# Order of slot and block products, first fetches, mix products and gate work in a graph and expert kernel

## What is computed

```
xn = layernorm(x)
h  = A @ xn                                # A: 3125 x 3125, sums edge weights (spmm)
z0 = softmax((A @ h)  @ W0.T + b0)         # 128 wide
z1 = softmax((A @ [z0, z0]) @ W1.T + b1)   # 128 wide
x  = x + tanh([z0, z1] + h) + mix(xn)      # mix: linear attention, q k v, per-head norms, wo
x  = x + ffn(layernorm(x))                 # 8 experts, gate picks one, capacity 489, 1024 hidden
```

## Time and profile before

| | us |
|---|---|
| median of 3 runs | 1150.28 |
| the profiled execution | 1142.74 |
| its span | 1141.0 |
| PE busy in the span | 1071.9 (94%) |
| PE's weight loads busy | 666.5 (58%) |
| DVE busy | 738.9 (65%) |
| ACT busy | 314.7 (28%) |
| POOL busy | 163.2 (14%) |
| first 25 iterations | about 15 to 216 |
| block products to their end | about 216 to 595 |
| layers 0 and 1 with the gate | about 600 to 902 |
| experts | about 913 to the end |

### The profile page before, as it was taken

How to read it: one execution, slowest core, us unless ns; L and a number is a source line. 1 busy time by engine, 2 the same in 40 slices (tenths; PEclk the granted TensorE clock), 3 DMA queues, 4 the chain that set the end, 5 groups by cost and what they waited for, 6 DMA issues and landing times.

```text
span 1141.0 us, 15390 instructions
## 1 busy us (share of the span) xinstructions
PE 1071.9 (94%) x5383; PEld 666.5 (58%) x5383; DVE 738.9 (65%) x1860; ACT 314.7 (28%) x1042; POOL 163.2 (14%) x208
## 2 busy tenths in 40 slices
PE   5869989999999999999979999999998799999995
PEld 3446656656666666666774444644458566666664
DVE  8978999998786887869950111217877445544444
ACT  4657867522222222222210111201112112222220
POOL 1113223301000000000000000000344511111111
PEclk9889999999999999999998999999999899999998
DMA  6111110111324333342348988987994665555510
GB/s 173 16 12 47 47 47 18 76 82 76 146 115 153 122 133 136 131 167 105 139 160 314 361 309 301 358 319 281 311 327 171 179 194 125 136 137 133 147 51 8
DMA packets 78877, 178.60 MB, mean 157 GB/s; under 512 B 33567, under 2 KB 62011, under 8 KB 66639
## 3 DMA queue, kind: packets, MB, share of 16 engines
q1 hardware_dynamic: 67550, 126.16, 34.4%
q10 hardware_dynamic: 7120, 43.34, 9.4%
q0 software_dynamic: 4128, 8.08, 2.0%
HBM read 116.23 MB, written 63.77 MB: 158 GB/s over the span
## 4 chain that ended last, share of the span: by engine, by line
PE 77%; DVE 11%; SPq 4%; issue 4%; ACT 2%; DMA 1%; POOLq 0%; POOL 0%; ACTq 0%; DVEq 0%
PE ps L1720 21%; PE ps L1571 20%; PE ps L1820 10%; PE ps L1808 9%; PE ps L1555 7%; SPq L477 2%; PE ps L1595 2%; PE ps L1530 2%; PE ps L1463 1%; PE ps L1516 1%; PE ps L1550 1%; DVE RING L1096 1%; DVE RING L1087 1%; DVE W L1039 1%; SPq L475 1%
## 5 line engine op out<-in xcount | busy, mean ns | idle before, releaser
L1571 PE MATMUL ps<-RING,XX 128*128 128x512 f32 (+2 forms) x700 | 297.1, 550 | 2.0 <-DVE W L1103 2.0
L1720 PE MATMUL ps<-RING,RY 128*128 128x512 f32 (+4 forms) x750 | 272.1, 520 | 5.7 <-issue 5.7
L1720 PEld LDWEIGHTS ps<-RING,RY 128*128 128x128 f32 x750 | 135.7, 194 | 125.7 <-issue 118.3
L790 ACT COPY RING<-ps 128x512 f32<-128x512 f32 (+3 forms) x163 | 91.0, 559 | 291.6 <-PE ps L1555 266.3
L1571 PEld LDWEIGHTS ps<-RING,XX 128*128 128x128 f32 x700 | 118.1, 191 | 69.9 <-issue 62.1
L1096 DVE TENSOR_TENSOR RING<-RING,RY 128x768 bf16<-128x768 bf16 x275 | 142.7, 560 | 4.0
L1555 PEld LDWEIGHTS ps<-RING 128*128 128x128 bf16 x1575 | 100.6, 97 | 50.0 <-issue 43.3
L1087 DVE TENSOR_TENSOR RING<-iota_p,RY 128x512 bf16<-128x512 bf16 x275 | 114.1, 456 | 18.1 <-PE ps L1555 15.7
L1555 PE MATMUL ps<-RING 128*128 128x128 bf16 (+1 forms) x1575 | 112.9, 217 | 0.0
L916 ACT ACTIVATE RY<-ps,b1T 128x489 f32<-128x489 f32 x64 | 42.8, 669 | 172.4 <-PE ps L1808 172.4
L1436 DVE SCALAR_TENSOR_TENSOR W<-ps,RING,W 128x256 f32<-128x256 f32 (+1 forms) x32 | 15.5, 484 | 99.0 <-PE ps L1820 97.8
(11 more groups left out here) (265 smaller groups left out, 1313.5 us busy)
## 6 DMA issues: line engine op xcount, KB each, us to landing
RING<-adj_dram SPq DMA_DIRECT2D x60, 1280.0 KB, 6.4
adj_dram<-RING ACTq DMA_DIRECT2D x30, 1280.0 KB, 4.8
rbuf_dram<-W SPq DMA_DIRECT2D x8, 516.0 KB, 5.1
RING<-rbuf_dram SPq DMA_DIRECT2D x8, 516.0 KB, 4.0
xbuf_dram<-W SPq DMA_DIRECT2D x8, 512.0 KB, 3.2
XT<-in_L_ffn_w SPq DMA_DIRECT2D x16, 256.0 KB, 5.2
XT<-in_L_ffn_w SPq DMA_DIRECT2D x4, 1024.0 KB, 8.6
RING<-in_L_ffn_w SPq DMA_DIRECT2D x16, 256.0 KB, 4.5
```

Of the source, the lines that this page charges most:

```text
L790: nc.scalar.copy(RING[:, n % 2, at:at + w], ps[:, u % 2, 0:w]).then_inc(s_bev, 1)
L1571: last = nc.tensor.matmul(ps[:, ACC + dd, 0:w], XN[:, j, dd * H:(dd + 1) * H], at[:, i * w:(i + 1) * w], start=(j == 0), stop=True, skip_g ...
L1720: last = nc.tensor.matmul(o, (Y if l == 0 else S0)[:, j, :], RING[:, slot_of[g % 5], i * across + first:i * across + first + w], start=(j ...
```

## The change

Six edits of order; no operation's size changes.
1. PE does slots(it-1) behind build(it-3), and kvprod ahead of turn. ACT's kept goes behind evac.
2. On SP's queue, five weight loads (wo, wq, W0, W1, b1) leave the place behind window group 1 and are issued by ACT in iteration 1; eleven small loads move from behind group 1 to behind group 2.
3. Mixes 16 to 24 (HELD = 16) come after the last block product, each in its own half bank; before, mixes 0 to 21 stood in the loop and 22 to 24 behind it. DVE's additions of these wait until a bank holds all its mixes, and come last. turns of layer 0, strips 0 and 1, wait for all additions.
4. ACT does zout(1, kc) ahead of exp8(ka) and xtout(kb).
5. In layer 1, counts(ka-1) and gate_turn(ka) leave strip kb for strip kc; turns(1, kb) and logits(ka) go from tiles 4 and 5 of strip kc to tile 13.
6. counts(ka) and gate_turn(kb) leave strip kc and follow turns(1, kc).

```diff
-MIX_AT = {40 + 4 * _m: _m for _m in range(NT - 3)}
+HELD = 16
+MIX_AT = {40 + 4 * _m: _m for _m in range(HELD)}
...
-        mix_bank = lambda m: MIXB if m < NT - 2 else ACC + m - (NT - 2)
+        HELD_AT = ((MIXB, 0), (MIXB, D), (KVACC, 0), (KVACC, D), (PROD, 0), (PROD, D), (ACC, 0), (ACC, D), (ACC + 1, 0))
+
+        def mix_out(m):
+            bank, at = HELD_AT[max(m - HELD, 0)]
+            return ps[:, bank, at:at + D]
+
+        def mixes_to_bank(m):
+            return m + 1 if m < HELD else max(n for n in range(HELD, NT) if HELD_AT[n - HELD][0] == HELD_AT[m - HELD][0]) + 1
...
-                if g == 1:
-                    for to, src in ((wo_n, half("L0_mix_wo")), (wq_n, half("L0_mix_wq")), (W0_n, a["L0_gnn_W0"]),
-                                    (W1_n, a["L0_gnn_W1"]), (b1_n, a["L0_ffn_b1"])):
-                        sp.dma_start(to, src).then_inc(s_wt5, 16)
+                if g == 2:
...
                 if it < NT:
                     turned(it)
+                if it == 1:
+                    for to, src in ((wo_n, half("L0_mix_wo")), (wq_n, half("L0_mix_wq")), (W0_n, a["L0_gnn_W0"]),
+                                    (W1_n, a["L0_gnn_W1"]), (b1_n, a["L0_ffn_b1"])):
+                        act.dma_start(to, src).then_inc(s_wt5, 16)
...
-                if 1 <= it <= NT:
-                    kept(it - 1)
                 if 0 <= u < NU:
                     evac(u)
...
+                if 1 <= it <= NT:
+                    kept(it - 1)
...
+            zout(1, kc)
             exp8(ka)
             xtout(kb)
-            zout(1, kc)
...
             def mixed(m):
-                dve.wait_ge(s_mixp, m + 1)
+                dve.wait_ge(s_mixp, mixes_to_bank(m))
                 dve.wait_ge(s_bo, m + 1)
-                v.tensor_tensor(X1[:, m, :], X1[:, m, :], ps[:, mix_bank(m), 0:D], ALU.add).then_inc(s_mrd, 1)
+                v.tensor_tensor(X1[:, m, :], X1[:, m, :], mix_out(m), ALU.add).then_inc(s_mrd, 1)
...
-            mixed(NT - 3)
             hn_out(NT - 2)
-            mixed(NT - 2)
             hn_out(NT - 1)
-            mixed(NT - 1)
+            for m in range(HELD, NT):
+                mixed(m)
...
-                if 1 <= it <= NT:
-                    slots(it - 1)
...
                     build(it - BUILD_IT)
+                if 1 <= it <= NT:
+                    slots(it - 1)
+                if KV_LAG <= it < NT + KV_LAG:
+                    kvprod(it - KV_LAG)
                 if it + 1 < NT:
                     turn(it + 1)
-                if KV_LAG <= it < NT + KV_LAG:
-                    kvprod(it - KV_LAG)
...
-            mix(NT - 3)
+            mix(HELD)
             hidden_node(NT - 2)
-            mix(NT - 2)
+            mix(HELD + 1)
             hidden_node(NT - 1)
-            mix(NT - 1)
+            for m in range(HELD + 2, NT):
+                mix(m)
...
+                if l == 0 and k < 2:
+                    pe.wait_ge(s_mrd, NT)
...
-            strip(1, kb, {3: [later(turns, 1, ka)], 4: [later(logits, ka - 1)], 14: [later(counts, ka - 1)], 22: [later(gate_turn, ka)]})
-            strip(1, kc, {4: [later(turns, 1, kb)], 5: [later(logits, ka)], 21: [later(counts, ka), later(gate_turn, kb)]})
+            strip(1, kb, {3: [later(turns, 1, ka)], 4: [later(logits, ka - 1)]})
+            strip(1, kc, {4: [later(counts, ka - 1)], 6: [later(gate_turn, ka)], 13: [later(turns, 1, kb), later(logits, ka)]})
             turns(1, kc)
+            counts(ka)
+            gate_turn(kb)
             logits(kb)
```

More of the change, by code:

```diff
@@ L1591, in mix @@
                 pe.wait_ge(s_mv, 1)
-                if m < NT - 2:
-                    ge(pe, s_mrd, m)
+                ge(pe, s_mrd, min(m, HELD))
                 for c in range(2):
-                    last = nc.tensor.matmul(ps[:, mix_bank(m), 0:D], XT[:, c, m * P:(m + 1) * P], M[:, c, :], start=(c == 0), stop=(c == 1))
+                    last = nc.tensor.matmul(mix_out(m), XT[:, c, m * P:(m + 1) * P], M[:, c, :], start=(c == 0), stop=(c == 1))
                 last.then_inc(s_mixp, 1)
```

## The result

The changed kernel takes 1136.47 us (median of 4 runs, 1133.77 to 1137.01) against 1150.36: ratio 0.9875, 95% interval 0.9855 to 0.9896, 13.9 us less. The prediction said 1137.3, 13.0 less.

A forecast was written before the change was run, and what follows sets the result against it. PE was taken as the bound, nearly full in the first 25 iterations and the long middle; 7.6 - 0.9 + 2.8 + 3.5 = 13.0 us off the 1150.28 median gave 1137.3, range 1133 to 1145.5.

The forecast's parts named there:

- (a): First fetches at the start: window group 2 is issued earlier and DVE's wait goes; 7.6 us, between 4 and 8.5.
- (b): Order in the first 25 iterations: build fills slots' waits, turn waits for kept; -0.9 us, between -4 and +2.5.
- (d): Gate work at the end of layer 1: the last biased(kc) starts 3.8 us earlier; taken as 3.5, between 1.5 and 4.5.
- 5.96: DVE's idle before head_scale at the start, expected to go with the earlier window group 2, bringing slots(5) 5.96 us earlier.
- 2.2 - 0.17: By product(7): build(3) no longer follows slots(5), 2.2 us won, less 0.17 for turn's new wait.
- the collision: ACT's five weight loads run beside window group 1's last windows; a delay of 0 to 1.7 us possible, 0.4 taken.
- rival 2: Starts collide, holding group 1's windows by 1.7, and small terms fall short: gain about 7 us, 1143.3; chance 0.21.
- a turn wait of 0.17: From product(7) to product(24), turn waits 0.17 for ACT's kept in each of 17 iterations: 2.9 us lost.
- The 0.33 at each chunk end: At four chunk ends ACT's store, issued ahead of kept, delays turn by 0.33 each: 1.3 us lost.
- (c): Mixes held back behind the block products: 1.3 us from a longer lead, 1.5 from the branch; 2.8, between 0 and 5.3.
- the drain of the chunk traffic: Behind the block products: chunk loads and stores end earlier relative to the branch on `rounds`, shortening it by 1.5 us.
- Rival 1: PE's sequencer could hold 32 pairs, so nearly all the 5.66 us gap goes: 2.5 us more, 1134.8; chance 0.10.

The follow-up runs named there:

- again: Changed kernel without any edit, run again on the second chip: 1127.58 us against 1142.90 for the kernel before, ratio 0.9859.
- five_sp: Changed kernel with the five weight loads back on SP's queue behind window group 1, second chip: 1126.51 us, ratio 0.9850.
- woven: The kernel both, with turn behind the first of apply's four matmuls from iteration 4 on: 1129.44 us, ratio 0.9818.
- held_only: Kernel before with only mixes 16 to 24 moved behind the last block product: 1145.96 us, ratio 0.9954.
- gate_only: Kernel before with only the moved gate work of layer 1's last strips: 1146.85 us, ratio 0.9965.
- after: First profiled execution of the changed kernel, span 1132.0 us; that kernel's median is 1136.47 us, ratio 0.9875.
- fetch_only: Kernel before with only the new order of first fetches (five weight loads, eleven small loads): 1148.12 us, ratio 0.9979.
- order_only: Kernel before with only the new order of the first 25 iterations (slots, kvprod, kept): 1147.74 us, ratio 0.9975.
- again2: Changed kernel without any edit, run a third time, on the third chip: 1136.31 us against 1151.26, ratio 0.9870.
- both: Changed kernel with the five weight loads back on SP and ACT's chunk store behind kept, third chip: 1133.02 us, ratio 0.9845.
- held20: Changed kernel with HELD = 20, so 12 pairs behind the last wait in place of 28: gap 4.94 us, no total time given.
- late_store: Changed kernel with ACT's chunk store issued behind kept and not ahead of it: 1125.07 us, ratio 0.9842.
- held18: Changed kernel with HELD = 18, so 20 pairs behind the last wait in place of 28: gap 3.12 us, no total time given.

## Why the prediction was right

The sum was 13.0; like for like (before against `again`) the spans differ by 14.7, and the medians by 13.9 to 15.3. The step that saved it was to take the 13.0 off the median shown and not off the profiled execution: the 7.5 between the two is the pause in strips kb and kc, which the change neither makes nor takes away (last section). That the total came this close is in part luck: (a) fell short, and (b), (d) and the clock made up for it.

**(a) and (b), 6.7 forecast, 6.65 measured** at kvprod(20), and 2.4 + 2.9 = 5.3 by the single parts. The sum is right and the terms were not. By product(7), where (a) was to end, 81.53 - 75.10 = 6.4 had come of 7.6. Little of that is the fetch, for which I had 5.96. Product(7) is at 79.7 to 79.8 in three kernels with the old order, one of them with the new fetches, at 76.85 with the new order alone, and at 74.7 to 75.5 with both (five profiles). So about 1.8 of the 6.4 was the lateness of the one profile of before, 2.9 the order (I had 2.2 - 0.17) and 1.3 to 2.1 the fetches on top of it. The 5.96 was one execution's wait (1.83 to 5.42 in three others), and the collision was sized at 0.4 where ACT's cast came 1.4 to 2.2 late. That was the first condition of rival 2, and my own mark for a wrong prediction, cast(1) after 26.5, was passed (27.07, 27.48); `five_sp` prices it at 1.0. The error of (b) went the other way: behind product(7) 0.2 was won where I had -0.9. I charged a turn wait of 0.17 in 17 iterations, 2.9 us; the wait is there (0.20, and with `woven`'s order the products come 0.18 closer), but the new order also brought build and slots 0.16 closer together, so an iteration grew by 0.05. That 0.16 I had nowhere in the sum. The 0.33 at each chunk end was right in kind: the rows have 0.51 to 0.54, of which 0.20 is the ordinary wait.

**(c), 2.8 forecast, 2.9 measured** for the gap (5.66 to 2.76), 5.3 (3.3 to 7.2) by the ratio of `held_only` alone. The mechanism held, the split did not: the lead grew by 2.3 (forecast 1.3), and from the load of `rounds` to the first strip it takes 6.74 in place of 7.33, 0.6 less (forecast 1.5). The branch took 6.2 to 7.0 us in the four kernels with the old mixes and 5.5 to 5.8 in the eight profiles with 28 pairs, so it does get shorter. My reason, the drain of the chunk traffic, fits the traces (last section), also the 6.9 with 12 pairs: that branch starts at 586.0, nearly as early as theirs, but its chunk store ends 6.6 us into it and theirs 2.6 to 2.8. No run tests it by itself. Rival 1, 32 pairs ahead, is out: 20 pairs do as well as 28.

**(d), 3.5 forecast, 4.5 measured** (13.55 - 10.17 = 3.4 by counts(5), 14.66 - 10.15 = 4.5 at the experts), 4.0 (2.6 to 5.5) by `gate_only`. As forecast, PE doesn't wait at counts(4), and biased(kc) at 877.22 starts 891.74 - 877.22 - 10.15 = 4.4 earlier behind strip ka; I had said 3.8 and taken 0.3 off for the clock, which wasn't needed. The rows of the first profile of after, read alone, said the opposite: biased(kc) at 882.97, 3.8 later by the same sum.

Between the first strip and counts(3) another 0.56 came, and 2.25 in after, through the clock (below); I had left that out.

## What to carry to other kernels

Where a profiled execution and the median differ by more than a few us, find the place before trusting the durations near it, and compare profiles milestone by milestone: two profiles that agree to 0.03 us for 850 us and then part show at once what is the chip's and what is the kernel's. A wait can stand in a trace without idle time: take the distance from start to start behind an order that is known to be free, as with the 0.45 and 0.65 here, and put one piece of independent work into it; then see by a later milestone whether the kernel keeps the gain, which `woven` did not between product(7) and product(24). Work held back ahead of a branch pays up to what the sequencer can run ahead, and no further.

## What the hardware showed

The pause. In nine profiles of eight kernels (after, whose chip isn't on record, and on the first and third chip fetch_only, order_only, held_only, gate_only, again2, both, woven, held20) counts(3) to the experts takes 53.9 to 56.0 us with the new gate order and 58.6 to 60.3 with the old; in the four on the second chip (again, five_sp, late_store, held18) 46.7 to 47.1 with the new, and 51.4 in before's own with the old. So it is some 8 us with either order. Each chip was seen in one stretch of time only, so that it is the chip is the likely reading, not shown. PE's rows run on at first, and those who wait for PE start some 4 us late (4.3 at gate_turn's copy). PE's sequencer is late as well: it reaches the wait ahead of turns(1, kb), at L1741, 0.8 us behind the start of counts(4) in `again` and 4.0 behind it in `again2`:

```profile
L1741 PEldq EVENT_SEMAPHORE  x2: 51/51/51, 867.4 to 871.7; - x2
...
L1741 PEldq EVENT_SEMAPHORE  x1: 51/51/51, 871.4 to 871.4; - x1
```

Of the 8.2 us between the two, 0.7 come by counts(4) and 4.1 more up to kc's last 22 matmuls. These take 3.64 in `again` and 6.06 in `again2`, where the granted clock was 0.50 from 874.1 to 880.2: 2.4 us of the pause are the clock's. What holds up PE's sequencer is open: no experiment was made on it.

The branch. The earlier trace rows have 6295 ns for a compare-and-branch that jumps over a long body, and PE's takes between 5.5 and 7.0 us in all 14 profiles. The DMA packets show what it waits for. In each profile one 16 KB packet of an instruction queue (q8) starts 3.2 to 4.6 us into the branch and takes 0.96 to 0.97, and the branch ends 1.36 to 1.39 us behind it. In `again` it is the one between 588.3 and 589.5 (packets, MB, share of 16 engines), and the branch ends at 590.78:

```profile
q8 instruction: 1, 0.02, 5.0%
```

So the branch is long because instructions are fetched in it, and its spread is how late that packet starts. The start goes with the chunk stores (q10). From the start of the branch to the packet these have, in `again` (585.12 to 588.43), before (594.07 to 598.03) and `held20` (586.02 to 590.56):

```profile
q10 hardware_dynamic: 65, 0.39, 28.1%
...
q10 hardware_dynamic: 103, 0.82, 48.9%
...
q10 hardware_dynamic: 115, 0.92, 47.7%
```

In the eight profiles with 28 pairs the last store ends 2.6 to 2.8 us into the branch and the packet starts at 3.2 to 3.5; in the other six it is 5.7 to 6.7 and 3.6 to 4.6. That the stores delay the packet isn't tested, and within the six the start varies with nothing that I can name. On SP, DVE and POOL the same line took 45 to 76 ns in the changed kernel, where they jump too. The Trainium skill (Advanced Engine Details and Errata, Control Flow Timing) has 108 ns: these three stay below it, and PE is far above it.

The lead. 18 pairs of weight load and matmul was the most that PE's sequencer was ahead at this place in any run. The Trainium skill (TensorE: Matmul & The Clock Gate) gives TensorE a queue of 64. If an entry is one load or one matmul of the trace, 28 pairs would have led further than 20 by it; the trace doesn't agree.

The clock. Behind a gap of about the same length PE started the first strip cold in one execution and warm in another. The windows are before, `again` and after, each from the start of its strip (length, busy PE, PEld, DVE, ACT, POOL, granted clock, DMA share, GB/s):

```profile
600.50:605.10 4.60, 4.57 (x6) 2.02 (x7) 0.00 (x0) 0.00 (x0) 0.00 (x0) 0.50 0.69 235
```

```profile
590.90:594.40 3.50, 3.46 (x4) 1.49 (x5) 0.00 (x0) 0.00 (x0) 0.00 (x0) 0.51 0.96 401
```

```profile
590.20:594.00 3.80, 3.80 (x9) 1.77 (x10) 0.00 (x0) 0.00 (x0) 0.00 (x0) 1.00 1.01 417
```

0.50 is the lower of the two levels, 1.2 GHz, 1.00 the upper. PE had stood 5.66, 2.76 and 2.79 us. From the first strip to counts(3) it took 261.40, 260.84 and 259.15: the cold start cost 2.25 and 1.7 us. A warm start isn't the end of it either: in `held_only`, `late_store`, `five_sp` and `woven` the clock was up as the first strip began and fell to 0.50 within 0.3 to 1.4 us, and all four took 260.84, as `again` did. Of the 14 profiles only after and `both` kept the upper level (259.15 and 259.14).
